# Head 0's small query and key stack loaded by six two-part transfers instead of twelve, ahead of the output's store

## The reference

```
att = einsum('bhid,bhjd->bhij', q, k) / sqrt(8)        # 16 heads of 8 channels, causal
S = relu(att[:, 0]); S[..., 0] = 0; S = S * (1 - eye)   # head 0 alone
FF = cumsum(S shifted by one row, axis=1)
att = att - FF[:, None]
keep = rank of FF (masked to causal) < min(budget - 1, i + 1), or the diagonal
y = softmax(where(keep, att, -inf)) @ v;  y @ w_proj.T + b_proj
ffn: 8 experts with a low-rank part each, the best 2 by a gate, relu between wi and wo
out = x + attention + ffn
```

## Time and profile before

| | |
|---|---|
| median of 3 executions | 663.17 us (660.14 to 664.04) |
| profiled execution | 660.72 us, its span 658.8 us, mean granted TensorE clock 0.967 |
| granted TensorE clock in 40 equal slices, tenths | 9655999999999999999999999998999999999999 (9 is 90% or more) |
| TensorE busy | 558.0 us, 85% of the span |
| VectorE busy | 507.2 us, 77% |
| GpSimd busy | 443.2 us, 67% |
| ScalarE busy | 373.7 us, 57% |
| DMA | 18.50 MB on the sync queue, 20.9% of 16 DMA engines |

### The profile page before, as it was taken

How to read it: one execution, slowest core, us unless ns; L and a number is a source line. 1 busy time by engine, 2 the same in 40 slices (tenths; PEclk the granted TensorE clock), 3 DMA queues, 4 the chain that set the end, 5 groups by cost and what they waited for, 6 DMA issues and landing times.

```text
span 658.8 us, 16724 instructions
## 1 busy us (share of the span) xinstructions
PE 558.0 (85%) x5431; PEld 380.9 (58%) x5431; DVE 507.2 (77%) x2173; ACT 373.7 (57%) x781; POOL 443.2 (67%) x740
## 2 busy tenths in 40 slices
PE   4647879889887998989888888989988899899994
PEld 1423545666466655656466655666566565676583
DVE  7878698757996789858997679858897689965351
ACT  3452676555765565664756555663757556455543
POOL 7518748695578856796478945797458965596451
PEclk9655999999999999999999999998999999999999
DMA  4152053135001520035000530025100450000000
GB/s 100 24 62 28 3 63 34 30 49 60 1 17 29 62 32 1 24 46 63 8 17 20 61 42 2 17 43 64 17 1 15 51 57 1 1 15 5 1 2 17
DMA packets 30070, 19.58 MB, mean 30 GB/s; under 512 B 6089, under 2 KB 29856, under 8 KB 29984
## 3 DMA queue, kind: packets, MB, share of 16 engines
q1 hardware_dynamic: 29984, 18.50, 20.9%
HBM read 3.22 MB, written 2.10 MB: 8 GB/s over the span
## 4 chain that ended last, share of the span: by engine, by line
PE 49%; DVE 19%; ACT 9%; POOL 9%; issue 8%; SPq 4%; DMA 1%; DVEq 1%; ACTq 0%; POOLq 0%
PE ps_t L900 12%; PE ps_o L919 9%; PE ps_s L887 7%; PE ps_m L832 6%; POOL ar L542 5%; DVE ar L1314 4%; SPq L405 4%; PE ps_m L844 4%; PE ps_m L828 3%; ACT pr L714 2%; ACT h L699 2%; ACT work L639 2%; POOL hsum L556 1%; PE ps_m L850 1%; ACT parts L568 1%
## 5 line engine op out<-in xcount | busy, mean ns | idle before, releaser
L542 POOL TENSOR_SCALAR ar<-ar,mx 128x512 f32<-128x512 f32 (+3 forms) x512 | 280.6, 560 | 174.7 <-DVE mx L1314 174.6
L1314 DVE CUSTOM_DVE_ANT_0 ar<-ps_s,mask 128x512 f32<-128x512 f32 (+3 forms) x512 | 230.9, 484 | 54.1 <-PE ps_s L887 52.8
L714 ACT ACTIVATE pr<-ps_t 128x512 f32<-128x512 f32 (+1 forms) x352 | 193.1, 558 | 108.7 <-PE ps_t L900 106.6
L900 PE MATMUL ps_t<-ident,ar 128*128 128x128 f32 x1280 | 202.2, 276 | 15.9 <-ACT pr L714 10.6
L900 PEld LDWEIGHTS ps_t<-ident,ar 128*128 128x128 f32 x1280 | 156.5, 142 | 54.0 <-issue 24.9
L887 PE MATMUL ps_s<-ks,qs 96*128 96x512 bf16 (+3 forms) x512 | 130.8, 308 | 17.3 <-DVE mx L1314 17.3
L919 PE MATMUL ps_o<-pr,va 128*32 128x128 f32 x2560 | 97.4, 279 | 6.0 <-ACT pr L714 5.6
L919 PEld LDWEIGHTS ps_o<-pr,va 128*32 128x32 f32 x2560 | 62.5, 110 | 45.9 <-ACT pr L714 28.6
L887 PEld LDWEIGHTS ps_s<-ks,qs 96*128 96x128 bf16 x512 | 43.3, 99 | 62.4 <-DVE mx L1314 31.1
L832 PE MATMUL ps_m<-zm,b_t 128*128 128x512 f32 x128 | 67.7, 610 | 8.4 <-ACT h L699 8.3
L699 ACT ACTIVATE h<-ps_m,bi_col 128x512 f32<-128x512 f32 x64 | 44.0, 687 | 53.8 <-PE ps_m L832 53.1
(11 more groups left out here) (220 smaller groups left out, 743.3 us busy)
## 6 DMA issues: line engine op xcount, KB each, us to landing
qs<-parts SPq DMA_DIRECT2D x42, 128.0 KB
ks<-parts SPq DMA_DIRECT2D x42, 128.0 KB
xs<-in_L_attn_x SPq DMA_DIRECT2D x8, 256.0 KB, 2.9
out<-res SPq DMA_DIRECT2D x8, 192.0 KB, 2.1
first_heads<-parts SPq DMA_DIRECT2D x72, 8.0 KB
qs<-parts SPq DMA_DIRECT2D x12, 64.0 KB
ks<-parts SPq DMA_DIRECT2D x12, 64.0 KB
out<-res SPq DMA_DIRECT2D x8, 64.0 KB, 12.9
```

Of the source, the lines that this page charges most:

```text
L542: nc.gpsimd.tensor_scalar(col, col, -1.0, mx[:, t % NA_RING, j:j + 1], ALU.mult, ALU.add)\
L714: nc.scalar.activation(pr[:, u % NP_RING, 0:w], ps_t[u % NT_RING][:, 0:w], ACT.Exp, scale=-1.0)\
L900: last = nc.tensor.transpose(ps_t[u % NT_RING][:, P * j:P * j + P], ar[:, u % NA_RING, P * j:P * j + P], ident[:, :])
L1314: nc.vector.tensor_tensor_reduce(out=ar[:, t % NA_RING, w * j:w * j + w], in0=ps_s[t % NS_RING][:, w * j:w * j + w], in1=mask[:, k % 2, OF ...
```

## The change

`make_first_heads` waits once, for both parts, and issues six transfers. Each takes the query part and the key part of one pair together: `parts` is seen as [rows, 6 parts, 512], of which two are picked by a stepped slice (part lo = Q_PART[j] and part hi = 3 + K_PART[j]), and they land side by side in 8 rows of `first_heads`, 16 KB in runs of 1 KB. The block moves ahead of the store of the batch's first three tiles in the queue. The counts that are waited for go from 192 to 96 a batch.

```
--- before.py
+++ after.py
@@ -398,12 +398,12 @@
                     def make_first_heads(m):
 
                         wait_full(sp, "s3", m - 1)
-                        for t in range(2):
-                            sp.wait_ge(split, 2 * m + t + 1)
-                            part = (Q_PART, K_PART)[t]
-                            for j in range(len(part)):
-                                sp.dma_start(first_heads[8 * j:8 * j + 8, t, :], parts[0:P:NH, t, part[j], :])\
-                                    .then_inc(topped, 16)
+                        sp.wait_ge(split, 2 * m + 2)
+                        for j in range(len(Q_PART)):
+                            lo, hi = Q_PART[j], 3 + K_PART[j]
+                            sp.dma_start(first_heads[8 * j:8 * j + 8, :, :],
+                                         parts[0:P:NH, :, :, :].rearrange("p t j c -> p (t j) c")[:, lo:hi + 1:hi - lo, :])\
+                                .then_inc(topped, 16)
 
                     fetch(0)
                     sp.dma_start(raw_attn, w_attn.rearrange("(t p) c -> p t c", p=P)).then_inc(w_first, 16)
@@ -435,13 +435,13 @@
                             store(sp, k - 1, 1)
                         if k + 3 < B:
                             fetch(k + 3)
-                        store(sp, k, 0)
                         if k + 2 < B:
                             make_first_heads(k + 2)
+                        store(sp, k, 0)
                     store(sp, B - 1, 1)
                     sp.wait_ge(stored, 32 * B)
                     sp.wait_ge(stacked, 192 * B)
-                    sp.wait_ge(topped, 192 * (B - 2))
+                    sp.wait_ge(topped, 96 * (B - 2))
                     sp.wait_ge(halved, 192)
 
                 @block.gpsimd
@@ -669,7 +669,7 @@
                                     act.wait_ge(stacked, 192 * n)
                                     act.wait_ge(halved, 192)
                                     if n >= 3:
-                                        act.wait_ge(topped, 192 * (n - 2))
+                                        act.wait_ge(topped, 96 * (n - 2))
                                 else:
                                     wait_read(act, "w_attn", 0)
                                 copy(qk32[:, j, :], m[:, :], name, n, False, bias=bqk_col[:, j:j + 1],
@@ -794,7 +794,7 @@
                                 last = nc.tensor.matmul(m[:, 0:T - P * j], head0[1][:, P * j:P * j + P],
                                                         head0[0][:, P * j:T], start=True, stop=True)
                             else:
-                                pe.wait_ge(topped, 192 * (n - 1))
+                                pe.wait_ge(topped, 96 * (n - 1))
                                 last = nc.tensor.matmul(m[:, 0:T - P * j], first_heads[:, 1, P * j:P * j + P],
                                                         first_heads[:, 0, P * j:T], start=True, stop=True)
                         elif name == "flag":
```

## The result

| | before | after |
|---|---|---|
| median of 4 executions | 662.09 us | 668.94 us (664.38 to 671.48) |
| ratio, 95% interval | | 1.0094, 1.0052 to 1.0135 |
| profiled execution, its span | 660.72, 658.8 us | 664.38, 662.5 us |
| mean granted TensorE clock | 0.967 | 0.958; the other three 0.950 to 0.952 |

What follows compares the result with a forecast made beforehand. No engine was taken to bound throughout; removing 11.0 us of small-stack waits would leave 5.6 us after GpSimd's backlog and 0.7 after the prefix sums, so 662.0 - 0.7 = 661.3 us, range 655.5 to 665.5.

Steps and rivals of the forecast that it cites:

- What bounds the kernel: Whole kernel: no engine bounds throughout; TensorE waits six times, 11.0 us in all, for head 0's small stack.
- the six transfers: Sync queue: six issues in place of twelve, each at a pitch of 0.60 to 0.65 us.
- the move: Block ahead of the store: first issue 0.8 us earlier, stack landed 3.0 us before s0 wants it.
- behind it in the queue: Store, big stack's twelve transfers and fetch, issued after the block: put at zero both ways.
- First step, GpSimd's backlog: Unit 2's transposes: TensorE waits for GpSimd's rows, keeping 0.7 us at four boundaries, 1.5 and 1.35 at two: 5.6 us.
- Second step, the prefix sums: VectorE's two scans: GpSimd, held by the first, delays s1's mask and the second; 0.7 us won in total (0 to 1.1).
- The sum: Whole kernel: the mean of four executions, 662.0, less 0.7 gives 661.3 us.
- the wait moves to zm and the clock falls: Gap before s3: TensorE's idle time gathers, clock falls at up to all six boundaries, +7.3 us, 669.3; chance 0.08.
- if the clock falls at more than one boundary: Batch boundaries: one of the stated signs, in the profile after, that the forecast is wrong.

Runs made afterwards that it cites:

- twelve-transfer: The kernel before with its twelve transfers moved ahead of the store: 665.61 us, ratio 1.0066.
- behind-the-store versions: The changed kernel's six two-part transfers, but issued behind the store as before: 664.73 us, ratio 1.0052.
- the kernel before with the later scan: The kernel before with the second prefix sum one slot later, behind unit 7's mask additions: 660.63 us, ratio 0.9971.
- the kernel before with the filling: The kernel before with the four transposes of the sixth unit of batches 1 to 6 done three times over: 665.50 us, ratio 1.0036.

## Why the prediction was wrong

*What bounds the kernel, the six transfers, the move, behind it in the queue:* right. There are 36 issues of 0.617 us; no wait is left; the twelve-transfer and the behind-the-store versions have the same waits to the tenth.

*First step, GpSimd's backlog:* right. TensorE waits for unit 2's rows, and once the mask is out of the way the earlier stack gives 4.9 us, where the slacks add up to 5.6.

*Second step, the prefix sums:* right in mechanism and place, too high in size. The unit behind the scans came at scan start + 3.45 (forecast 3.3 to 3.47), zm's wait at s3 grew from 0.8 to 1.73 (forecast 1.5 or more), and the work of a boundary changed by +0.06 us in all for the forecast 0.7 (0.21 lost four times, not 0.1; 0.45 won twice, not 0.5 to 0.55). The Trainium skill (SBUF — State Buffer, Who interferes with whom) has the starter hold the shared pair to its end. The trace agrees, and better than I had worked it out: the scan waits out the multiplication in flight. Before and after, at the same boundary:

```profile
369.47 0.95 POOL L542 TENSOR_SCALAR ar<-ar,mx 128x256 f32<-128x256 f32 x2
...
370.02 1.53 DVE L1061 TENSOR_TENSOR_SCAN ft<-ones,s 128x511 f32<-128x511 f32 x1
```

```profile
373.23 1.84 POOL L542 TENSOR_SCALAR ar<-ar,mx 128x256 f32<-128x256 f32 x2
...
373.51 1.28 DVE L1061 TENSOR_TENSOR_SCAN ft<-ones,s 128x511 f32<-128x511 f32 x1
```

Before, the second of two multiplications had 0.40 us to run (to 370.42) and the scan took 0.40 + 1.13; after, the first had 0.20 to run (373.23 + 0.48) and the scan took 0.20 + 1.08. So the rule cost nothing on top of before, where I had it cost 0.15 a boundary: the waiting out was in the old rows already, and was longer there.

*The sum:* this is where it failed. It has no term for the clock: "the wait moves to zm and the clock falls" was a rival with a chance of 0.08, put at nothing in the sum. Its mechanism is what happened, and its sign of being wrong, "if the clock falls at more than one boundary", came true. Two things were wrong with its working. I took "the idle stretches of 1.6 to 2.4 at the old wait left the clock at full" as evidence against, though the old wait is at another place, ahead of s0. Length alone does not decide: in the kernel before TensorE stood idle for 2.35 us up to 213.2 at full clock, longer than any gap ahead of s3. A longer one at s0 can do it too: in the kernel before with the later scan the small stack came late once, TensorE's matmuls waited 2.88 us, and

```profile
210.00:213.20 3.20, 0.59 (x7) 0.99 0.20 49
213.20:216.60 3.40, 3.13 (x9) 0.50 0.59 63
```

The runs with gaps of 1.97, 1.55 and 1.09 us ahead of s3 have mean clocks of 0.954, 0.959 and 0.966. And I priced it from one profile, where a fall is a matter of the execution: the mean over executions has 12.6 us more at half clock, which is about 6 us, where the sum has nothing. The rival's own figure with falls at all six boundaries, 669.3, lies near the measured 668.94 by luck: the profiles have falls at two or three of six, and all four with the gap of 1.97 us have one more at 577 to 582. The measured median of 668.94 comes from four executions; twelve more of the same kernel have 665.95, still past the end of the range (665.5).

The price of a fall was about right: 76.4 - 75.1 = 1.3 us for a batch with one, where the rival took 1.6.

What stays open: why the gap of 1.97 us is followed by a fall at the first two or three boundaries of an execution and not at the later ones; why a gap ahead of s3 does it more easily than one ahead of s0; the fall at 569 to 582 us, in all profiles in which the small stack comes early but the three that have the gap filled threefold, which is a quarter of the 12.6 us; two falls at 256 and 257 us; and the long half of the executions of the kernel before with the filling.

## What to carry to other kernels

When a wait is taken away, follow the won time to the next place at which all engines meet, and price not only how long the engine stands still there but in how many pieces: the same idle time in one gap can cost more than the change won. The order of small instructions in a full queue matters: one mask of 0.3 us, moved ahead of two multiplications, is what let the earlier stack pay (655.14 us; with the mask moved and the filling, but the twelve transfers left behind the store, it is 662.14). Where a change makes one of TensorE's waits longer, compare the mean granted clock over many executions before and after, since a single profile can't show it.

## What the runs showed of the hardware

- More TensorE work made the kernel faster: 0.9 us of repeated transposes in a gap of 1.97 us took the mean granted clock from 0.954 to 0.966 and the median from 665.95 to 660.64.
- The clock fell at the end or within 2.1 us of 14 of 36 gaps of 1.30 to 1.97 us ahead of s3, and of 1 of 48 of 1.09 us and less (14 profiles). Of the 24 waits of 1.5 to 2.9 us for the small stack ahead of s0 (four profiles) it fell at two, those of 2.47 and 2.88 us.
- Time against time at half clock, over the 12 executions of the changed kernel: 0.5 us lost for each microsecond at half clock, as if TensorE were the bound throughout, though no engine is. Over the executions of the kernel before it is 0.3 to 0.4.
- VectorE's prefix sum and GpSimd's multiplications and mask exclude each other, and each waits out the one in flight: the first scan of 511 columns took 1.07 to 1.14 us beyond the rest of GpSimd's instruction (0.20 to 0.48 us) at all twelve boundaries of the two kernels, and GpSimd's next instruction 0.9 to 1.0 us more than its own time.
